# New orders for a two-layer graph kernel, and every second one-hot comparison of its lookup on GpSimd

## The reference, cut to what matters

```python
# layer 0, four blocks
sq = jnp.sum(xyz * xyz, axis=1)
d2 = sq[:, :, None] + sq[:, None, :] - 2.0 * jnp.einsum('bdn,bdm->bnm', xyz, xyz)
_, idx = jax.lax.top_k(-d2, K)                       # K = 8
for i in range(NUM_BLOCKS):
    shortcut = points
    p = _lrelu(points)
    g = _group_point(p, idx_t)                       # the 8 neighbours' columns
    c = jnp.einsum('oi,bin->bon', w_center[i], p)
    gn = jnp.einsum('oi,bikn->bokn', w_neighbor[i], g)
    points = (c + gn.sum(axis=2)) / (K + 1.0) + shortcut
# layer 1
idx = _knn(x_loc, 30)
rel = pts[bidx, idx] - pts[:, :, None, :]            # first 3 features of ctx
feat = [rho, theta, phi, each minus their mean]      # of rel
h = lrelu(_bn(feat @ W1.T, g1, b1))                  # 6 -> 6
h = lrelu(_bn(h @ W2.T, g2, b2))                     # 6 -> 3
h = lrelu(_bn(h @ W3.T, g3, b3))                     # 3 -> 1
att = jax.nn.softmax(h[..., 0], axis=-1)             # over the 30 neighbours
agg = jnp.einsum('bnkc,bnk->bnc', xk, att)
return x + agg.transpose(0, 2, 1)
```

## Time and profile before

| | us |
|---|---|
| median of 3 runs (lowest, highest) | 841.17 (841.12, 841.86) |
| the profiled execution | 846.98 |
| its span | 845.1 |
| PE busy | 749.7 (89%) |
| DVE busy | 656.1 (78%) |
| ACT busy | 260.7 (31%) |
| POOL busy | 175.3 (21%) |
| mean granted clock of PE | 0.949 of full speed |

### The profile page before, as it was taken

One profiled execution on the slowest core, in us unless ns is written; L12 is line 12 of the kernel. 1 busy time (PEld: TensorE's weight loads), 2 busy tenths in 40 slices (PEclk: granted clock), 3 DMA queues, 4 the chain that ended last, 5 costly groups with the idle time before them and its releaser, 6 DMA issues.

```text
span 845.1 us, 13319 instructions
## 1 busy us (share of the span) xinstructions
PE 749.7 (89%) x5530; PEld 611.5 (72%) x5530; DVE 656.1 (78%) x1057; ACT 260.7 (31%) x367; POOL 175.3 (21%) x134
## 2 busy tenths in 40 slices
PE   5979899698999999789899959794988999898988
PEld 3768788677778888678688747573876887676766
DVE  4757987969899999798897899677667878786701
ACT  7325642421551212100011221121232545454500
POOL 3113855861403113002200220121040000000000
PEclk9889899899999999999899998796999999999999
DMA  9520002020002000444430000000000455848581
GB/s 358 143 99 2 1 1 100 1 100 0 1 1 100 0 1 1 186 168 145 136 125 2 0 1 0 1 1 0 0 1 2 161 201 175 285 145 291 185 300 56
DMA packets 32700, 73.43 MB, mean 87 GB/s; under 512 B 11392, under 2 KB 11392, under 8 KB 30336
## 3 DMA queue, kind: packets, MB, share of 16 engines
q1 hardware_dynamic: 32496, 70.49, 23.9%
q10 hardware_dynamic: 144, 2.10, 0.6%
HBM read 49.37 MB, written 23.20 MB: 86 GB/s over the span
## 4 chain that ended last, share of the span: by engine, by line
PE 38%; DVE 37%; DMA 9%; ACT 7%; issue 6%; POOL 2%; SPq 0%; ACTq 0%; DVEq 0%; POOLq 0%
PE bank L1389 11%; DMA att_d<-scratch 6%; DVE scratch L937 5%; DVE idx L813 4%; DVE vals L811 4%; DVE scratch L881 3%; DVE pts_l L886 3%; PE bank L1417 3%; PE bank L1287 2%; PE bank L1368 2%; PE bank L1288 2%; PE bank L1289 2%; PE bank L1477 2%; PE bank L1369 2%; PE bank L1370 2%
## 5 line engine op out<-in xcount | busy, mean ns | idle before, releaser
L1389 PE MATMUL bank<-nbr,pts_l 128*128 128x512 f32 x1024 | 246.5, 399 | 10.5 <-DVE pts_l L886 8.2
L1389 PEld LDWEIGHTS bank<-nbr,pts_l 128*128 128x128 f32 x1024 | 194.5, 192 | 53.7 <-DVE pts_l L886 10.4
L461 POOL TENSOR_TENSOR pts_h<-scratch,pts_h 128x512 fp32r<-128x512 f32 x58 | 81.6, 1410 | 354.6 <-ACT pts_h L635 354.6
L1368 PE MATMUL bank<-wT,pts_h 128*128 128x512 f32 x256 | 105.7, 413 | 9.9 <-DVE pts_l L886 9.9
L635 ACT CAST pts_h<-scratch 128x512 fp32r<-128x512 f32 x58 | 35.9, 620 | 236.9 <-DVE scratch L881 236.9
L1369 PE MATMUL bank<-wT,pts_h 128*128 128x512 f32 x256 | 102.7, 401 | 0.0
L1370 PE MATMUL bank<-wT,pts_h 128*128 128x512 f32 x256 | 102.6, 401 | 0.0
L720 ACT COPY scratch<-bank 128x512 f32<-128x512 f32 x64 | 69.9, 1135 | 68.7 <-DMA att_d<-scratch 45.2
L1287 PE MATMUL bank<-pts_h 128*128 128x512 f32 (+2 forms) x192 | 74.5, 388 | 15.4 <-DVE pts_l L784 11.7
L642 ACT CAST pts_l<-bank 128x512 fp32r<-128x512 f32 x64 | 37.2, 588 | 135.9 <-PE bank L1370 135.7
L1288 PE MATMUL bank<-pts_l,pts_h 128*128 128x512 f32 (+2 forms) x192 | 71.0, 370 | 0.0
(11 more groups left out here) (189 smaller groups left out, 1214.4 us busy)
## 6 DMA issues: line engine op xcount, KB each, us to landing
att_d<-scratch SPq DMA_DIRECT2D x64, 256.0 KB, 2.5
nbr<-att_d SPq DMA_DIRECT2D x16, 1024.0 KB, 7.1
more<-a_rows SPq DMA_DIRECT2D x17, 480.0 KB, 4.5
scratch<-a_rows SPq DMA_DIRECT2D x15, 480.0 KB, 4.2
X<-in_ctx SPq DMA_DIRECT2D x12, 512.0 KB, 7.7
out_dram<-X SPq DMA_DIRECT2D x16, 256.0 KB, 4.6
more<-in_ctx SPq DMA_DIRECT2D x4, 512.0 KB, 7.8
scratch<-in_fside_BxSxS SPq DMA_DIRECT2D x2, 1024.0 KB, 13.5
```

The lines of the kernel that those rows point to most:

```text
L461: pool.tensor_tensor(p_l[:, t, hf * HALF:(hf + 1) * HALF], p32(n), p_h[:, t, hf * HALF:(hf + 1) * HALF].bitcast(F32), ALU.subtract).then_i ...
L1368: pe.matmul(bank[g % 3][:], p_h[:, t, cols], wT[:, 0, t, :], start=(t == 0), stop=False)
L1389: mm = pe.matmul(bank[3 + g % 3][:], y[:, m, t * P:(t + 1) * P], nbr[b][:, m, hf * HALF:(hf + 1) * HALF], start=(m == 0 and part_ == 0), s ...
```

## The change

The work is the same; where it stands in the lists of the engines is not.

1. Ahead of the slots: PE puts `gram(2)` before `adj_turn(0)`. ACT moves several calls, among them `p_high(0..3)`, which now stand behind `gram_out(13)`, `mirror_out(13)` and `gram_out(14)`, and `adjacency(6)`, `(7)`, now behind `mirror_out(14)`. DVE puts the first two selection steps of tiles 6 and 7 behind the first four `p_make`.
2. The index rows move from slots 47, 51, 55, 59 to 36, 39, 42, 52, and PE and ACT take them one slot later. SP stores rows 0 to 2 ahead of all broadcasts. `lookup` now waits for all four.
3. The odd half tiles are compared on POOL, with a semaphore of their own.
4. The network takes 42 slots and not 38, with empty slots ahead of items 24, 37 and 44, each of which now shares its slot with the item behind it. `T0` goes from 109 to 113 and `S0` from 115 to 119, so that `S_END` goes from 26 to 18, and `LOAD_AT` follows from them.

```diff
             + [(T, n) for Q in range(NT, TILES, 2) for n in range(3, STEPS) for T in (Q, Q + 1)]
-        R0 = 47
+        ROWS_AT = {36: 0, 39: 1, 42: 2, 52: 3}
+        TURN_AT = {g + 1: c for g, c in ROWS_AT.items()}
...
-        NET = [(0,), (1,), (2,), (3, 4), ((5, 0),), ((5, 1), (5, 2)), (6,), (7,), (8, (9, 0)), ((9, 1),),
...
+        NET = [(0,), (1,), (2,), (3, 4), ((5, 0),), ((5, 1),), ((5, 2),), (6,), (7,), (8,), ((9, 0),), ((9, 1),),
+               ((9, 2), 10), (11,), (12, 13), (14,), (15,), (16,), (17,), (18,), (19,), (20,), (21,), (22,), (),
+               (24, 25), (26,), (27, 28), (29, 30), (31, 32), (33, 34), (35,), (), (37, 38), (39,), (40,), (41, 42),
+               (), (44, 45), (46,), (47,), (48,)]
...
             for c in range(CHUNKS):
-                sp.wait_ge(s_ar, c + 1)
-                sp.dma_start(a_rows[c], a_row[:]).then_inc(s_arow, 16)
-                sp.wait_ge(s_arow, 16 * (c + 1))
+                if c < CHUNKS - 1:
+                    sp.wait_ge(s_ar, c + 1)
+                    sp.dma_start(a_rows[c], a_row[:]).then_inc(s_arow, 16)
...
+            def onehot_a(u):
+                pool.wait_ge(s_bc[u % NB], 16 * (u // NB + 1))
+                pool.tensor_scalar(bc[u % NB], bc[u % NB], part[:, 0:1], None, ALU.is_equal).then_inc(s_oh[1], 1)
...
+                    if G0 <= g < G0 + TILES:
+                        onehot_a(2 * (g - G0) + 1)
...
             act.wait_ge(s_g, NT + 3)
+            gram_out(13)
+            mirror_out(13)
+            gram_out(14)
             for j in range(CT):
                 p_high(j)
-            gram_out(13)
+            mirror_out(14)
             adjacency(6)
-            mirror_out(13)
-            gram_out(14)
             adjacency(7)
-            mirror_out(14)
...
-            select([6, 7], 0, 2)
             dve.wait_ge(s_prm, 16 * (9 + 6 * B))
...
             for n in range(CT):
                 p_make(n)
-            select([6, 7], 2, 3)
+            select([6, 7], 0, 3)
...
-                for u in (2 * (g - G0), 2 * (g - G0) + 1):
-                    if 0 <= u < 2 * TILES:
-                        onehot_a(u)
+                if G0 <= g < G0 + TILES:
+                    onehot_a(2 * (g - G0))
...
-                pe.wait_ge(s_oh, u + 1)
+                pe.wait_ge(s_oh[u % 2], u // 2 + 1)
...
-                pe.wait_ge(s_ar, row_turned(G0 + 1 + u // 2))
+                pe.wait_ge(s_ar, CHUNKS)
```

More of the change, by code:

```diff
@@ L214, in build @@
         s_bc = [sem(f"a_broadcast{i}") for i in range(NB)]
-        s_oh = sem("onehot_ready")
+        s_oh = [sem("even_onehot_ready"), sem("odd_onehot_ready")]
         s_look = sem("lookup_done")
@@ L287, in w_bank @@
             return bank[(6, 7, 4, 5, 0, 2, 6, 7)[n]][:]
-        def row_turned(g):
-            return min(max((g - R0 - 2) // 4 + 1, 0), CHUNKS)
         @block.sync
@@ L337, in _ @@
             sp.wait_ge(s_sel, NT + 4)
-            sp.wait_ge(s_adjT, TILES)
-            sp.wait_ge(s_sel, TILES)
             for c in range(CHUNKS):
-                sp.wait_ge(s_ar, c + 1)
-                sp.dma_start(a_rows[c], a_row[:]).then_inc(s_arow, 16)
-                sp.wait_ge(s_arow, 16 * (c + 1))
+                if c < CHUNKS - 1:
+                    sp.wait_ge(s_ar, c + 1)
+                    sp.dma_start(a_rows[c], a_row[:]).then_inc(s_arow, 16)
+            for c in range(CHUNKS):
                 for t in range(2 * CH):
                     u = 2 * CH * c + t
+                    if u == 0:
+                        sp.wait_ge(s_arow, 16 * (CHUNKS - 1))
                     if u == 3:
                         sp.wait_ge(s_sel, TILES)
+                    if u == 9:
+                        sp.wait_ge(s_ar, CHUNKS)
+                        sp.dma_start(a_rows[CHUNKS - 1], a_row[:]).then_inc(s_arow, 16)
+                    if u == 2 * CH * (CHUNKS - 1):
+                        sp.wait_ge(s_arow, 16 * CHUNKS)
                     if u >= NB:
@@ L588, in _ @@
             nbr_out(0)
+            adjacency(1)
             mirror_out(2)
-            adjacency(1)
             gram_out(3)
@@ L605, in _ @@
             gram_out(6)
-            nbr_out(2)
             for k in range(KT):
@@ L610, in _ @@
             gram_out(7)
+            nbr_out(2)
             adjacency(3)
@@ L619, in _ @@
             gram_out(9)
+            mirror_out(9)
             adjacency(4)
-            mirror_out(9)
+            adjacency(5)
+            gram_out(10)
+            mirror_out(10)
             nbr_out(4)
-            gram_out(10)
-            adjacency(5)
-            mirror_out(10)
             gram_out(11)
             mirror_out(11)
-            norm_out(1)
             nbr_out(5)
             gram_out(12)
+            norm_out(1)
             mirror_out(12)
@@ L665, in side @@
                     nbr_out(T)
-                if (g - R0) % 4 == 2 and 0 <= (g - R0) // 4 < CHUNKS:
-                    a_row_out((g - R0) // 4)
+                if g in TURN_AT:
+                    a_row_out(TURN_AT[g])
                 if g == 16 + NT:
@@ L899, in index_rows @@
                 src = idx[:, CH * c:CH * (c + 1), :].rearrange("p t k -> p (t k)")
+                dve.wait_ge(s_sel, CH * (c + 1))
                 if c:
@@ L909, in onehot_a @@
                 dve.wait_ge(s_bc[u % NB], 16 * (u // NB + 1))
-                dve.tensor_scalar(bc[u % NB], bc[u % NB], part[:, 0:1], None, ALU.is_equal) \
-                    .then_inc(s_oh, 1)
+                dve.tensor_scalar(bc[u % NB], bc[u % NB], part[:, 0:1], None, ALU.is_equal).then_inc(s_oh[0], 1)
             def pick_r(u):
@@ L1158, in side @@
                     select_step(T, n)
-                if (g - R0) % 4 == 0 and 0 <= (g - R0) // 4 < CHUNKS:
-                    index_rows((g - R0) // 4)
-                for u in (2 * (g - G0), 2 * (g - G0) + 1):
-                    if 0 <= u < 2 * TILES:
-                        onehot_a(u)
+                if g in ROWS_AT:
+                    index_rows(ROWS_AT[g])
+                if G0 <= g < G0 + TILES:
+                    onehot_a(2 * (g - G0))
                 for u in (2 * (g - G0) - 4, 2 * (g - G0) - 3):
@@ L1331, in _ @@
                 w_turn(n)
+            gram(2)
             adj_turn(0)
-            gram(2)
             gram(3)
@@ L1399, in turn_a @@
                     pe.wait_ge(s_nbr, TILES)
-                u = min(2 * (R0 + 4 * c - G0), 2 * TILES - 2)
-                if u >= 0:
-                    pe.wait_ge(s_pick, u + 1)
                 pe.transpose(bank[6][:, 384:HALF], a_f, ident[:]).then_inc(s_aT, 1)
             def lookup(u):
-                pe.wait_ge(s_oh, u + 1)
+                pe.wait_ge(s_oh[u % 2], u // 2 + 1)
                 if u == 0:
@@ L1433, in side @@
                     adj_turn(T)
-                if (g - R0) % 4 == 2 and 0 <= (g - R0) // 4 < CHUNKS:
-                    turn_a((g - R0) // 4)
+                if g in TURN_AT:
+                    turn_a(TURN_AT[g])
                 for u in (2 * (g - G0) - 2, 2 * (g - G0) - 1):
```

3 lines of the change are left out of this document (removed).

## The result

The changed kernel is slower: 866.39 us median (865.32 to 866.88), against 841.51 (841.12 to 843.53) of the kernel before on the same chip, a ratio of 1.0285 (95% interval 1.025 to 1.032). The profiled execution took 865.32 us, of which 863.2 are span.

| stage | before | after | change | predicted |
|---|---|---|---|---|
| to slot 0 | 175.5 | 167.1 | -8.4 | -7 |
| slots 0 to 51 | 171.5 | 172.8 | +1.3 | +1 |
| lookup, to slot 69 | 108.1 | 124.6 | +16.5 | -11 |
| network, to slot 111 | 183.2 | 163.9 | -19.3 | -21 |
| slots 112 to 127 | 72.3 | 63.2 | -9.0 | +2 |

The account below looks back on a forecast made before the run. DVE paced slots 0 to 51, PE the lookup, mutual waits of PE and DVE the network, the HBM round trip the tail. Terms -7 + 1 - 11 - 21 + 2 + 33 gave -3 to -4 from 841.17: 837.5 us, range 825 to 851.

Parts of the forecast that it names:

- the price of a comparison on POOL: Lookup: one odd comparison on POOL was taken at 2.2 us, bounds 1.8 and 4.35, hidden in a slot of some 6.
- The second rival: Lookup: the comparison on POOL holds DVE or runs long, so -2 in place of -11, 847 us; chance 0.13.
- the 97 forecast: Lookup, 108.1 us before: PE's waits for index rows and the first one-hot go, -11, with PE's 96.0 as floor.
- Ahead of slot 0: Start: PE's idle 6.59 us goes as ACT copies first; -7, bounds -10 and -4.
- Slots 0 to 51: DVE-bound before and after, three calls of `index_rows` instead of two: +1.
- Network: Slots 70 to 111: PE's 12.3 us wait for statistics and DVE's waits behind it go; -21 after 1 for shared slots.
- Slots 112 to 127: Last slots: column transposes fall here, +7, and eight spreads fewer, -5; together +2.
- The 7 us for the column transposes: Slots 112 to 127: transposes with their copy on ACT, where DVE waited 7.54 us, now fall here, +7.
- Tail: After slot 127: spreads +4.5, chunk starts +28, cold clock +9.6, stores -9; +33, from +25 to +56.
- the four starts: Tail: PE waits at each chunk's start for a copy and its last load, 7.3, 6.6 twice and 7.5; together 28.
- eight spreads and the cold clock: Tail: eight spreads come back, +4.5, and PE runs cold after each start, 2.4 us each, 9.6.
- what fewer bunched loads give: Tail: with one load per four stores, 9 of 22 us were taken as gone, bounds 0 and 13.

Follow-up runs that it names:

- e1: The changed kernel with all comparisons back on DVE and the new orders kept: 843.46 us, ratio 1.0011.
- e6: The changed kernel with each comparison on POOL cut into four pieces of 480 columns: 859.37 us, ratio 1.0223.
- e8: The changed kernel with all comparisons on DVE, plus four 480-column comparisons on POOL in each of sixteen slots whose output nobody reads: 855.56 us, ratio 1.0177.
- e5: The changed kernel with the odd comparisons on ACT as two activations instead of on POOL: 843.50 us, ratio 1.0009.
- e2: The kernel before with only the odd comparisons moved to POOL: 870.53 us, ratio 1.0366.
- e3: The kernel before with only the new network table (42 slots, spreads four slots later): 855.01 us, ratio 1.0168.
- e7: The changed kernel with only the last 480 of 1920 columns of each odd comparison on POOL, the rest on DVE: 839.58 us, ratio 0.9982.
- e11: The changed kernel with all comparisons on DVE and each load of a quarter issued one spread sooner: 842.99 us, ratio 1.0011.
- e4: The changed kernel with all comparisons on DVE and the network in 40 slots: 819.46 us, ratio 0.9749.
- e9: The changed kernel with the network in 40 slots and only a quarter of each odd comparison on POOL, the rest on DVE: 813.13 us, ratio 0.9660.

## Why the prediction was wrong

**The step that failed** is the price of a comparison on POOL: "So the upper bound is 15 x 0.29 = 4.35 us, and the lower ... 1.8 us. The cast is the nearest kind, most of it fixed cost as the iotas show; I take 2.2". It takes 5.1 us at least, above my upper bound. The rows that would have been right were there: an elementwise operation of POOL on 512 columns takes 1.3 to 1.7 us (rows 6 has one), 2.5 ns or more a column with all that is fixed, and the comparison takes 5.11 us over 1920, 2.66. I took the input count for what sets the rate, and an iota, which reads nothing, for the slope. The Trainium skill points the same way as I did ("GPSIMD Engine Reference", Engine selection: one-input operations run at roughly line rate there, two-input ones about twice as slow as on DVE). Here the one-input comparison costs as much a column as the two-input `p_low`, and seven times DVE's 0.71 us for 1920; the measurement decides.

**The second rival was right in kind and too small.** It gave back 9 us of the gain, for POOL's own list alone. With 5.2 us the comparisons and `p_low` fill POOL's aggregation slots (it is busy for 48 of 54 us from 373 to 427 us), and DVE is held for some 41 us in all. The rival also looked at too few slots. It priced the eight aggregation slots alone; of the 25.1 us over e1 these have 7.1, while slots 52 to 55 have 9.1 and slots 64 to 69 have 8.9. Freed of the comparisons (e1) the lookup takes 99.5 us, close to the 97 forecast without them: of the miss of 27.5 us in this stage, 25.1 are POOL's. e6 and e8 show that neither way alone makes it. The Trainium skill's rule on the shared port pair ("SBUF — State Buffer", Who interferes with whom), which I had cited and then not put into the sum, is borne out: a DVE instruction waits for up to one whole comparison of POOL. L926 takes 983 ns on average here, 323 with the comparisons in pieces and 279 in e5. In e1 and in the kernel before, where POOL has only `p_low` in these slots, it is 555 and 518, so `p_low` holds it too.

**Ahead of slot 0** -8.4 for -7, or some -6 against e2 and e3. The way is in part the one foretold: the idle 6.59 us of rows 2 are gone, and what is late next is POOL's `p_low`, for which PE's first product waits 4.0 us. The cold clock is not gone: from 155 to 160 us PE again runs at 0.50.

```profile
PE bank L1377 <- POOL pts_h L470: 4.0, 1, 4.0
```

**Slots 0 to 51** +1.3 for +1.

**Network** -19.3 for -21: PE's 12.3 us for the statistics are 0.2. e3 has the same -19.3 with nothing else changed.

**Slots 112 to 127** -9.0 for +2, the second miss, 11 us to the good side. The 7 us for the column transposes were wrong. I had counted DVE's 7.54 us wait before slot 111 as a cost of PE that moves. In the profile after, slots 111 to 119 take 22.1 us (31.1 before), which is PE's pace of 2.7 us a slot; 4.6 of the difference are the eight spreads. The rest, about 4.4 us, I put down to DVE's index columns, which no longer stand ahead of aggregations that PE has to wait with; that was only argued. And part of the -9.0 is luck with the clock. With the same lists these slots took 67.6 us in e1 at a clock of 0.92, 64.2 to 65.8 in e3, e5, e6, e7, e8 and e11 at 0.95 to 0.97, and 63.2 in the changed kernel's profile at 1.00.

**Tail** +37.0 for +33, by its terms: the four starts 31.5 us (28 predicted; the copy and the load cost what they were priced at or less, 1.1 and 5.6, but the last copies came late, because at the first three starts a store before them stood 4.3 to 5.2 us behind the load before), eight spreads and the cold clock 11.3 us more of PE's busy time (132.6 against 121.2; 14.1 predicted), and what is left of the stage gave back 5.8 us, the old wait of 2.5 among them (9 predicted, as what fewer bunched loads give; no run takes that term by itself). That the starts are the cause e4 shows: with one attend over them most of the loss is gone.

**The sum.** Take e1's 25.1 us off the +18.1 and the span would have moved by -7. e1, which is that kernel, moved by -1.8 us of span and by nothing in time: it has the lookup of 99.5, but its last slots are 4.4 us longer than in this profile. So without the comparison the edits are no change within the noise, near the -3.5 forecast, and in part by luck, since the other terms' misses (+4 in the tail, -11 in the last slots, +2 in the network, -1 ahead) partly cancel. What made the kernel slower is the one term whose bounds did not hold.

## What to carry to other kernels

An operation that moves to GpSimd is priced by the nearest elementwise operation *of that engine* by element count, and its length counts twice: on what stands behind it in that engine's list, and on DVE, which it can hold for one whole instruction. Pieces alone gave back 11.7 of the 25.1 us (e6); with a quarter of the work, 1.5 us a slot, nothing was lost (e7, e9).

A transfer that must land before a stage starts needs work over it, counted in time at its latest issue. Making the spreads four slots later took away the eight that had stood over each last load, and turned one short wait into four of 8 us, each with a cold clock behind it; half the move (e4) kept most of the network's gain and left one wait of 2.7 us.

## What was not expected of the hardware

POOL's comparison of bf16 against a scalar costs 2.53 ns a column, somewhat more than the 2.2 ns between its two-input fp32 operations of 512 and 1024 columns (1.28 and 2.40 us), and 0.26 us an instruction. Two activations of 1920 columns on ACT take 1.90 us each, and DVE's `pick_r` beside them took 285 ns at most. A GpSimd that is busy for 103 of 111 us need not hold DVE (e8). A load of 1 MB that was never bunched landed in 4.9 to 6.6 us, median 5.6, against 7.1 and up to 9.6 before.
